# Fused adaLN attention and tile-routed FFN on one core: output summed in DRAM, y normalised on ScalarE, shorter calibration, new setup

## The reference, cut to what matters

```
x2  = x + gate(ga) * attention(LN(x)*(1+ca) + sa)         # signed scores, causal softmax
h2  = LN(x2)*(1+cb) + sb
cluster = argmax(calibrate(h2 @ cluster_sigs.T))           # 8 clusters
tile    = argmax over the 8 tiles of that cluster of calibrate(h2 @ sigs.T)
y   = h2 + direction[tile] * spline_tile(tanh(gelu(h2@W1+b1)@W2+b2)) * output_scale
out = x2 + gate(gb) * (LN(y)*gamma + beta)
```

## Time and profile before

| | us |
|---|---|
| median of 3 runs | 472.15 (471.57 to 474.82) |
| the profiled execution, its own time | 471.67 |
| its span, first to last instruction | 469.8 |
| PE busy | 399.8 (85%) |
| DVE busy | 398.5 (85%) |
| ACT busy | 296.5 (63%) |
| POOL busy | 67.4 (14%) |

### The profile page before, as it was taken

One profiled execution on the slowest core, in us unless ns is written; L12 is line 12 of the kernel. 1 busy time (PEld: TensorE's weight loads), 2 busy tenths in 40 slices (PEclk: granted clock), 3 DMA queues, 4 the chain that ended last, 5 costly groups with the idle time before them and its releaser, 6 DMA issues.

```text
span 469.8 us, 7656 instructions
## 1 busy us (share of the span) xinstructions
PE 399.8 (85%) x2072; PEld 308.7 (66%) x2072; DVE 398.5 (85%) x1367; ACT 296.5 (63%) x645; POOL 67.4 (14%) x82
## 2 busy tenths in 40 slices
PE   2697899999999999899989998999899999463330
PEld 2555578777777877687768776877677778452220
DVE  4417637387859899999999999999999899999996
ACT  2230365877698769676967697769776976651400
POOL 1002310302020002400250015001400220031040
PEclk9977899999999999999999999999999999796565
DMA  8503102101200213112310231122100210040112
GB/s 292 142 30 105 74 23 79 35 1 45 69 23 1 69 45 114 45 28 86 114 45 25 91 112 47 22 91 86 50 1 1 73 64 1 4 130 0 35 57 89
DMA packets 26234, 28.72 MB, mean 61 GB/s; under 512 B 3888, under 2 KB 21552, under 8 KB 26192
## 3 DMA queue, kind: packets, MB, share of 16 engines
q1 hardware_dynamic: 24160, 26.38, 17.8%
q10 hardware_dynamic: 2032, 1.85, 1.2%
HBM read 19.77 MB, written 8.45 MB: 60 GB/s over the span
## 4 chain that ended last, share of the span: by engine, by line
DVE 45%; PE 42%; issue 8%; ACTq 2%; ACT 2%; DVEq 0%
PE bank L511 8%; PE bank L530 8%; PE bank L490 6%; PE bank L500 6%; PE bank L553 3%; DVE y L1278 3%; DVE y L1246 3%; DVE x L1091 3%; DVE res L1288 3%; DVE st L1254 2%; DVE probs L1077 2%; DVE st L1046 2%; PE bank L520 2%; ACTq L680 2%; DVE v L1070 2%
## 5 line engine op out<-in xcount | busy, mean ns | idle before, releaser
L511 PE MATMUL bank<-h,g 128*128 128x128 f32 (+3 forms) x256 | 80.2, 444 | 4.9 <-DVE v L1070 4.9
L978 POOL TENSOR_TENSOR res<-x,gb_row 128x512 f32<-128x512 f32 x32 | 44.5, 1407 | 268.3 <-DMA out<-res 268.3
L530 PE MATMUL bank<-v,probsT 128*128 128x257 f32 x320 | 79.1, 382 | 0.0
L500 PE MATMUL bank<-m_ga,h 128*128 128x258 f32 x256 | 68.8, 394 | 5.2 <-DVE rows L1360 3.2
L530 PEld LDWEIGHTS bank<-v,probsT 128*128 128x128 f32 x320 | 57.1, 190 | 6.6 <-DVE y L1246 0.3
L490 PE MATMUL bank<-h,a_sb 128*128 128x512 f32 x128 | 60.4, 595 | 0.0
L511 PEld LDWEIGHTS bank<-h,g 128*128 128x128 f32 x256 | 44.7, 195 | 22.1 <-issue 8.5
L500 PEld LDWEIGHTS bank<-m_ga,h 128*128 128x128 f32 x256 | 47.7, 197 | 15.7 <-issue 4.3
L736 ACT ACTIVATE bank<-bank,v 128x128 f32<-128x128 f32 (+1 forms) x64 | 31.7, 495 | 41.4 <-PE bank L511 29.1
L1077 DVE CUSTOM_DVE_ANT_0 probs<-bank,cmask 128x128 f32<-128x128 f32 (+1 forms) x64 | 31.1, 485 | 23.3 <-ACT bank L736 23.3
L742 ACT ACTIVATE probs<-probs,negmax 128x128 f32<-128x128 f32 (+1 forms) x64 | 35.5, 557 | 5.9 <-DVE negmax L1077 5.9
(11 more groups left out here) (167 smaller groups left out, 770.1 us busy)
## 6 DMA issues: line engine op xcount, KB each, us to landing
x<-in_L_attn_x SPq DMA_DIRECT2D x16, 512.0 KB, 3.5
out<-res SPq DMA_DIRECT2D x16, 512.0 KB, 3.0
a_row<-gate_rows SPq DMA_DIRECT2D x16, 256.0 KB, 3.2
gb_row<-gate_rows SPq DMA_DIRECT2D x16, 256.0 KB, 3.2
wide<-in_L_wmod ACTq DMA_DIRECT2D x2, 768.0 KB, 7.6
res<-in_L_attn_Wq SPq DMA_DIRECT2D x1, 256.0 KB, 5.0
res<-in_L_attn_Wk SPq DMA_DIRECT2D x1, 256.0 KB, 7.3
res<-in_L_attn_Wo SPq DMA_DIRECT2D x1, 256.0 KB, 10.1
```

Of the source, the lines that this page charges most:

```text
L500: last = mm(ps[:, 0:VW], h[s][:, c, t * P:(t + 1) * P], m_ga[p % 2][s][:, c, :], start=(c == 0), stop=(c == KC - 1))
L511: last = mm(ps[:, 0:w], g[s][:, c, t * P:(t + 1) * P], h[s][:, c, 0:w], start=(c == 0), stop=(c == KC - 1))
L530: last = mm(ps[:, 0:D + 1], probsT[s][t][:, j * P:(j + 1) * P], v_sb[s][:, j, 0:D + 1], start=(j == 0), stop=(j == t))
L978: gp.tensor_tensor(res[:, 2 * u:2 * u + 2, :], x2[p % 2][s][:, t, :], gb_row[p % 2][s][:, 1:2, :].broadcast_to([P, 2, D]), ALU.add).then_i ...
```

## The change

All orders are written anew, and the `step` and `ahead` helpers are gone. In words:

- **Output in DRAM.** SP writes the beta rows (gb times beta) of the first 14 batches straight from `gate_rows` over the whole output (`dma_beta`, 7168 rows of 1 KB, DRAM to DRAM). POOL then issues two accumulating transfers for each batch: x2 from SBUF (`ax`), and later the finished y (`ay`), 28 in all. `base`, `oa`, `ob` and `res` are left for the last two batches only.
- **y.** ACT normalises it (`yh`, in place), DVE multiplies with the gb row (`yg`). y has two buffers. y_ waits until the accumulation of y of two groups before has landed, b_x2 the same for x2.
- **Calibration** in ten steps. The segment is found by rounding; a line per knot segment is formed (448 columns: times slope, plus knot, times mark), and one reduction of 448 columns to 64 ends it.
- **Groups.** From the LN of x2 on the kernel goes by groups: seven pairs, then the last two batches alone (groups 7 and 8, four tiles each).
- **Setup.** c is turned before its silu; ga of batches 0 and 1 is computed on 128 partitions directly (`su_gax`, `sd_gax`); the signature constants are made on POOL; the ACT loads go to SP, the bias loads to POOL; wmod comes in three parts; half of the first xhat and h is made on DVE.

```diff
+            def dma_beta():
+                spq.wait_ge(gb_sent, 16)
+                n_ = before(BY_DVE)
+                spq.dma_start(out[0:n_], gate_rows[0:n_, 3 * D:4 * D].unsqueeze(1).broadcast_to([n_, S, D])).then_inc(beta_sent, 16)
...
+            def su_gax(b):
+
+                pe.wait_ge(in_mod_ga, 16)
+                pe.wait_ge(cT_rdy, 1)
+                mod_rows(free(f"su_gax{b}", (ga_own[b], 1)), 2, P,
+                         lambda c: c_T[:, c, b:b + 1].broadcast_to([P, P])).then_inc(ga_two[b], 1)
...
+            def yh(g, t):
+                act.wait_ge(ln3_ready, g + 1)
+                own = y[g % 2][:, t, :]
+                A(own, own, ACT.Identity, bias=ln3["nmr"][:, t:t + 1],
+                  scale=ln3["rstd"][:, t:t + 1]).then_inc(yhat_rdy, 1)
...
+            def ax(g, i):
+                (p, s) = of_group(g, i)
+                pool.wait_ge(beta_sent, 16)
+                pool.wait_ge(x2_rdy, NT * (before(g) + i + 1))
+                gp.dma_start(out_v[GROUPS[g][i]], x2[p % 2][s][:, :, :], accum_op=ALU.add).then_inc(x2_sent[p % 2][s], 16)
+
+            def ay(g, i):
+                pool.wait_ge(scaled_rdy, NT * (before(g) + i + 1))
+                pool.wait_ge(x2_sent[g % 2][i], 16 * (g // 2 + 1))
+                gp.dma_start(out_v[GROUPS[g][i]], y[g % 2][:, NT * i:NT * (i + 1), :], accum_op=ALU.add).then_inc(summed[g % 2][i], 16)
...
-                need(dve, base_rdy, NT * (p - 2) + 2 * s + t // 2 + 1)
+                need(dve, x2_sent[p % 2][s], 16 * (p // 2))
...
+                    m(tt(own, by_segment(low), by_score(steps[:, 0:K1]), ALU.is_equal))
...
+                    m(tt(line, by_segment(back), by_score(knot_lin[:, 1, :]), ALU.mult))
...
+                    m(tt(line, line, by_score(knot_lin[:, 0, :]), ALU.add))
...
+                    m(tt(line, line, own, ALU.mult))
...
+                    m(red(val[:, 0:n_], line, X, ALU.add))
...
+                need(dve, summed[g % 2][t // NT], 16 * (g // 2))
...
+            def yg(g, t):
+                dve.wait_ge(yhat_rdy, NT * before(g) + t + 1)
+                if t % NT == 0:
+                    dve.wait_ge(gb_ld[g % 2][t // NT], 16 * gb_uses(g, t // NT))
+                own = y[g % 2][:, t, :]
+                tt(own, own, gb_row[g % 2][t // NT][:, 0, :], ALU.mult).then_inc(scaled_rdy, 1)
```

More of the change, by code:

```diff
@@ L232, in prev, with before, tiles, user @@
             return NT * seq(p - 1, s) + NT
[L234 to L246, removed]
+        def before(g):
+            return GROUPS[g][0] if 0 <= g < len(GROUPS) else B if g > 0 else 0
+        def tiles(g):
+            return NT * len(GROUPS[g])
+        def user(g, slot):
+            return min(before(g), before(g - 1) + slot + 1) if g > 0 else 0
+        def fs_units(g):
+            return ((0, 1, 2), (3, 4, 5), (6, 7)) if tiles(g) == PT else ((0, 1), (2, 3))
+        def fs_before(g):
+            return sum(len(fs_units(i)) for i in range(max(g, 0)))
+        def gb_uses(g, i):
+            return sum(1 for j in range(g % 2, g + 1, 2) if i < len(GROUPS[j]))
+        def stat(g):
+            first = NT * (GROUPS[g][0] % 2)
+            return slice(first, first + tiles(g))
+        def of_group(g, i):
+            return GROUPS[g][i] // 2, GROUPS[g][i] % 2
         @block.sync
         def _(spq):
-            def col(a):
-                return a.rearrange("(c p) -> p c", p=P)
             def row(a, n):
@@ new lines, in _ @@
+            for i in range(1, 3):
+                y_st(0, i)
+            b_v(3, 0, 0)
+            y_(0, 4)
+            a_st(4, 0, 0)
+            b_ttr(2, 1, 3)
+            b_ri(2, 1, 1)
+            y_(0, 5)
+            b_st(2, 0, 3)
+            y_st(0, 3)
+            loc(1, 0)
+            b_x2(2, 1, 1)
+            y_st(0, 4)
+            y_(0, 6)
+            loc(1, 1)
+            y_(0, 7)
+            b_st(2, 1, 0)
+            b_ri(2, 1, 2)
+            b_st(2, 1, 1)
+            loc(1, 2)
@@ new lines, in _ @@
+            b_st(6, 1, 2)
+            b_x2(6, 1, 3)
+            loc(5, 4)
+            b_st(6, 1, 3)
+            b_v(7, 0, 0)
+            loc(5, 5)
+            c_var(6, 0)
+            y_st(4, 5)
+            for i in range(1, 4):
+                c_var(6, i)
+            loc(5, 6)
+            y_st(4, 6)
+            b_v(7, 0, 1)
+            c_b2(5)
+            c_nw(6, 0)
+            loc(5, 7)
+            for i in range(1, 4):
+                c_nw(6, i)
+            loc(5, 8)
+            b_ttr(7, 0, 0)
@@ new lines, in _ @@
+            for i in range(4, 6):
+                y_(5, i)
+            y_st(5, 3)
+            y_(5, 6)
+            y_st(5, 4)
+            y_(5, 7)
+            lob(6, 3)
+            b_ri(7, 1, 1)
+            b_st(7, 1, 0)
+            lob(6, 4)
+            b_x2(7, 1, 1)
+            y_st(5, 5)
+            oh(6, 0)
+            y_st(5, 6)
+            oh(6, 1)
+            y_st(5, 7)
+            clc(7, 0)
+            y_var(5, 0)
+            clc(7, 1)
+            yg(4, 4)
+            y_var(5, 1)
@@ L1548 @@
+            oa(8, 3)
+            for i in range(0, 4):
+                ob(8, i)
 _INS = ['L0_attn_x', 'L0_attn_Wq', 'L0_attn_bq', 'L0_attn_Wk', 'L0_attn_bk', 'L0_attn_Wv', 'L0_attn_bv', 'L0_attn_Wo',
```

2944 lines of the change are left out of this document (2130 added, 814 removed), and 16 rows, old and new, of the table BANK.

## The result

The changed kernel takes **561.37 us** (median of 4 runs, 560.66 to 565.09); the kernel before took 471.86 beside it (470.38 to 474.82). The ratio is 1.190, 95% interval 1.183 to 1.198: slower by 19%, where the forecast was 441 and faster. The profiled execution has a span of 558.8 us. A run over 1.5% above the fastest of its kernel is left out of the ratios: one of e3's four, and two of the 13 of the kernel before that ran beside e9 to e11.

What follows compares the result with a forecast made beforehand. It took PE (pairs 1 and 2), DVE (pairs 3 to 6) and a DVE tail as bounds after a slow start; 74 + 315 + 50 = 439 us of span, 441 with 1.9 outside it, range 425 to 460.

Steps and rivals of the forecast that it cites:

- Term 1: Setup up to pair 1: 78.8 us becomes 74, with the first V_ at 29 and a_row waiting behind the big transfer.
- The 7.34 MB go at the rate of the setup's loads: Setup, beta transfer on SP's queue: priced at 300 GB/s, 24.5 us, ending at 64.5.
- my upper bound: Setup: if reading and writing DRAM halves the transfer's rate, 24.5 us more, so pair 1 begins at 98.
- The estimate by the engine count: Setup: 14 batches outermost would use 14 DMA engines of 16, making the transfer 28 us and the total 3.5 longer.
- The rival with the full gain: Setup: the big transfer is done before its followers matter or runs faster; 74 becomes 67, total 434 us; chance 0.20.
- Term 2: Middle, the steady pairs: 321.2 us becomes 315, DVE falling to 40.3 a pair and PE becoming the bound.
- ACT gains 8 yh at 0.602 - 0.08, 4.2 on 36.5: 40.7: Middle: ACT's normalisations of y add 4.2 us a pair, leaving ACT at 40.7, under PE's 45.8.
- the work that now stands ahead of the last AT: End of the middle: the front of batch 14's FFN and some gather of pair 6, about 3 us moved from the tail.
- Term 3: Tail: 69.8 us becomes 50, with 42.5 of DVE work, 4 of gaps and 3.4 for the last output.
- DVE or ACT stays the bound: Middle: POOL's descriptors hold DVE, or ACT drops behind, giving back 8.9 us and a little; total 452; chance 0.14.
- Half rate: Setup: the big transfer runs at half the rate, 98 us for 74, total 465; chance 0.09.
- The slower case: Middle: the accumulating transfers, estimated at 6 to 9 us each, become the bound; at 13.5 each, total 498; chance 0.08.

Runs made afterwards that it cites:

- e3: Changed kernel with ACT tables loaded only when the next function needs the other one, and beta sent in seven pieces behind pair 1's loads: 500.34 us (1.060).
- e9: e6 without beta and with x2 written plainly instead of accumulated (output lacks beta): 456.51 us (0.969).
- e11: Changed kernel with ACT's tables kept and the one big beta transfer at its place, read from beta rows of 4 KB: 473.93 us (1.004).
- e4: Changed kernel with the big transfer reading x, one contiguous source, instead of beta rows: 518.64 us in one run.
- e8: Changed kernel with the big transfer reading 7168 different 1 KB rows of x, tokens outermost: 521.62 us in one run.
- e7: Changed kernel with the big transfer from the same 14 beta rows of 1 KB, but tokens outermost: 560.33 us in one run.
- e6: e3 with each batch's beta sent as 128 rows of 4 KB, read from a row holding beta four times: 457.81 us (0.973).
- e1: Changed kernel with an ACT table loaded only when the next function needs the other one, the preload behind Tanh gone: 513.48 us (1.089).
- e12: e6 with ACT's normalisation of y cut from 256 columns to one: 457.56 us (0.970).
- e10: e9 with y's transfers written plainly too (output is y alone): 454.57 us (0.965).
- e2: Changed kernel with beta sent in seven pieces behind the loads that pair 1 needs, instead of one transfer: 547.01 us (1.162).

## Why the prediction was wrong

The span was forecast at 439 and is 558.8. By the three terms, to the same cut: the start is 41 us too long, the middle 64.8, the tail 14.1.

**Term 1, setup: the queue was read rightly; the failed step is "The 7.34 MB go at the rate of the setup's loads", 24.5 us.** The first V_ came at 26.0 (forecast 29). a_row10 did wait behind the big transfer, as said. But I priced 7.34 MB at 300 GB/s, from loads that read different rows, and my upper bound was half the rate, V_(1) at 98. It came at 114.95: at 112 to 139 GB/s the rate was under half. The bound was taken from "reading and writing DRAM", which e4 and e8 show to cost little here (28.6 us in e8), and not from what was special in this transfer, 512 reads of each of 14 rows (e7 against e8: 66.7 us). A second step was missing: SP stood still for 59 us with the x loads of pair 2 in its list too, and they, not a_row, ended the wait for V_(1), 3.9 us later in the changed kernel and 4.5 in e11. The estimate by the engine count, 3.5 us for 14 engines against 16, would not have saved it either: e7 undid the 14 and gained nothing. The rival with the full gain, V_(1) at 67, is what e6 gives (64.4).

**Term 2, middle: the failed step is "ACT gains 8 yh at 0.602 - 0.08, 4.2 on 36.5: 40.7".** It counted the instructions that the code adds and none of those that the new order brings in. The 40.7 is what ACT takes once the tables are kept (40.18 in e1); the changed kernel has 7 x 1.283 = 9.0 on top, 48.90. I had looked at POOL, DVE and the queues for what the moved steps do, and not at the order of Gelu and Tanh on ACT, where two of the table loads already stood in the trace of before. This is worth the 47.9 us of e1. The other steps held: DVE 39.06 (40.3), PE the bound at 46.1 a pair (45.3) in e1, e3, e6 and e12.

What is left is seen in e6, whose pairs 1 to 7 stand in windows cut as before:

```profile
64.43:100.34 35.91, 35.62 (x173) 26.28 (x174) 21.59 (x79) 24.40 (x55) 7.37 (x6) 1.00 0.41 89
100.34:147.66 47.32, 47.22 (x251) 36.13 (x250) 37.04 (x131) 40.08 (x85) 5.11 (x4) 1.00 0.40 93
147.66:199.13 51.47, 51.21 (x280) 40.41 (x279) 43.00 (x162) 43.80 (x92) 5.11 (x4) 1.00 0.37 79
199.13:245.20 46.07, 45.98 (x249) 35.73 (x248) 39.42 (x152) 40.06 (x89) 7.67 (x6) 1.00 0.56 115
...
337.60:397.90 60.30, 55.45 (x290) 43.36 (x289) 49.62 (x191) 46.27 (x105) 6.43 (x5) 0.92 0.34 55
397.90:456.50 58.60, 18.44 (x83) 14.80 (x81) 50.54 (x183) 25.28 (x58) 10.25 (x8) 0.54 0.40 71
```

The middle is 333.5 here, 17 more than the forecast's 315 and the 1.6 of the other cut. Pair 1 is 6.3 shorter than in the earlier trace rows and pair 2 1.5 longer; pair 3 has 280 PE instructions for 245 and takes 6.2 more than 45.3; pairs 4 to 6 take 0.8 to 1.0 more each, 2.6. The largest piece is pair 7, 60.3 for about 48: I gave the work that now stands ahead of the last AT 3 us, and it is some 50 PE instructions: PE is busy for 55.45 us with 290 of them, before for 44.79 with 241, and it idles for another 4.9. Which of them PE waits for there I did not try apart.

**Term 3, tail: 58.6 in e6, 62.5 in the changed kernel, for 48.4 to the same cut.** DVE has 50.5 us of work where I counted 42.5. The group of yg after the last AT in e6:

```profile
L2079 DVE TENSOR_TENSOR y<-y,gb_row 128x256 f32<-128x256 f32 x16 | 8.6, 546 | 0.1
```

yg takes 546 ns on average, not 417, and that mean is one long instruction among short ones: 2.48 us at 428.30, the others near 0.42. The timeline has a second such step, with the POOL instruction beside it:

```profile
420.31 2.32 DVE L1963 TENSOR_TENSOR lin<-lin,knot_lin 128x224 f32<-128x224 f32 x1
```
```profile
420.57 1.81 POOL L1763 TENSOR_TENSOR res<-x,gb_row 128x512 f32<-128x512 f32 x1
```

Elsewhere in the tail that step takes 0.39 us. POOL still adds x2 and beta (base, 1763) for the last two batches, at 420.57, 428.72 and 446.50; beside the first stands this step, beside the second the long yg, and beside the third a narrow step of 1.23 us at 447.78. Together they are 5.1 us over their kind. The earlier trace rows had shown what DVE loses beside base; I had struck that off with the base of the other batches. A transfer that POOL issues without a base behind it, at 413.23, has no such step beside it. No run without the base was made, so this rests on the rows that lie side by side, three times out of three. The other 3 us are not assigned.

**The rivals.** "DVE or ACT stays the bound" named the right engine at the wrong size (452). "Half rate" was nearest for the transfer. The slower case was looked for in the accumulating transfers; the estimate of 6 to 9 us for them was right (6.3 to 6.5), and from e6 to e10 the medians fall by 3.2 us for them and beta together, which is not clear of the noise. Slower came true by two causes of which the prediction had the one too cheap and the other not at all. They add: the tables bring 47.9 us alone (e1) and 46.7 on top of the pieces (e2 to e3), and from e1 to e6 the transfer brings 55.7 more. In e11 not only the end of the queue's chain came out but its parts: the ga rows landed at 69.7, where the sum has 69.6 (64.5 + 3.5 + 1.6).

## What to carry to other kernels

Where the order on ScalarE changes, write down its functions in order with the table that each needs, and count the loads; a preload only helps until the next function that its table lacks. Price a transfer by its nearest kin in source and shape as well as in bytes: a broadcast read from a few DRAM rows by many engines has a rate of its own, and an outermost dimension of two left most DMA engines idle here. Follow every load behind a large transfer on the same queue to whoever needs it, not only the first. Large transfers that nobody waits for yet belong behind the small ones that somebody does.

## What the runs showed of the hardware

- 7.34 MB from DRAM to DRAM in rows of 1 KB: 28.6 us from 7168 different rows, 66.7 from 14 rows read 512 times each (e8, e7). From 14 rows of 4 KB, read 128 times each, 282 GB/s (e11). From a piece's two rows of 1 KB, 47 GB/s at a DMA share of 0.14 (e3), per busy engine as fast as e8.
- A transfer of 7168 rows held the queue that issued it: one issue instruction behind it took 54.7 us in the changed kernel and 20.0 in e8. The four loads at that place took 13.17 in e11 (1792 rows of 4 KB) and 2.31 in e4 (one contiguous source).
- Once issued, a small transfer behind a large one still lands late: the 32 KB of the ga rows took 9.4 us in the changed kernel, 16.8 in e11 and 19.2 in e4, and 1.6 where they went out alone.
- An accumulating 512 KB transfer from POOL lands after 6.3 to 6.5 us (medians of the changed kernel; up to 8.0 in e3), a plain one from POOL after 4.6 to 4.8, a plain one from SP after 3.0.
- An ACT instruction on one column takes 382 ns, one on 256 columns 593 (e12, e6).
- A table load is 1.283 us of ACT, and in a kernel where ACT is the bound 47 fewer of them gave back 47.9 us (e1).
- Beside an addition on POOL of 1.8 us, single DVE instructions took 2.3 to 2.5 us instead of 0.4 (e6).
